# VectorE adds and masks the slot numbers, one operation a pair, and TensorE sums them two units earlier

## The reference

```
off = xn @ W_off + b_off ; w = softmax(xn @ W_attn + b_attn over 4 points)   # 8 heads x 4 points
idx = clip(off as an index into 128 features of the sequence's first token)
attention = broadcast(sum over heads and points of x0[idx] * w) @ W_out + b_out
ffn = sum over 2 shared experts of (silu(x w1) * (x w3)) w2
    + sum over the token's best 2 of 8 routed experts, weighted by a softmax of their two logits
```

## Time and profile before

| | us |
|---|---|
| median of three runs | 412.9 |
| the profiled execution's own time | 413.27 |
| its span | 411.3 |
| TensorE busy in the span | 367.9 |
| VectorE busy | 317.6 |
| ScalarE busy | 189.0 |
| GpSimd busy | 225.8 |

### The profile page before, as it was taken

The page is one execution under the profiler, slowest core; times in us unless marked ns, Lnnn a source line. Parts: engine busy times, 40 slices in busy tenths (PEclk is TensorE's granted clock), DMA queues, the critical chain, the costliest instruction groups (busy, mean ns, idle before and its releaser), DMA issues.

```text
span 411.3 us, 12487 instructions
## 1 busy us (share of the span) xinstructions
PE 367.9 (89%) x4333; PEld 317.0 (77%) x4333; DVE 317.6 (77%) x864; ACT 189.0 (46%) x446; POOL 225.8 (55%) x184
## 2 busy tenths in 40 slices
PE   0067798889999999999999999999999999999992
PEld 0065565467667777777779999999999999999992
DVE  5978989977966799999996778866666666666662
ACT  2778728395432466667666444322222222222220
POOL 0434500403777777343301999448876667766676
PEclk9999999899999999999999999999999999999998
DMA  8944630000117299988885456686854654543233
GB/s 291 297 112 103 119 89 0 2 0 16 49 53 150 73 182 184 171 167 178 141 124 102 121 180 175 164 77 72 76 60 58 60 74 57 61 56 35 27 34 33
DMA packets 98870, 41.35 MB, mean 101 GB/s; under 512 B 73600, under 2 KB 92416, under 8 KB 98816
## 3 DMA queue, kind: packets, MB, share of 16 engines
q1 hardware_dynamic: 87120, 31.82, 38.0%
q0 software_dynamic: 11264, 8.69, 16.5%
q10 hardware_dynamic: 432, 0.11, 0.2%
HBM read 10.93 MB, written 12.88 MB: 58 GB/s over the span
## 4 chain that ended last, share of the span: by engine, by line
PE 75%; DVE 11%; ACT 5%; DMA 3%; issue 2%; SPq 2%; POOL 1%; POOLq 0%; DVEq 0%; ACTq 0%
PE pY L835 18%; PE pY L668 11%; PE pAB L811 8%; PE pAB L810 8%; PE pAB L809 8%; PE pAB L656 5%; PE pAB L658 5%; PE pAB L657 5%; PE pV L680 3%; ACT units L888 2%; PE pV L626 2%; ACT wsp L960 2%; DVE hbuf L1226 1%; DVE hot L1132 1%; DMA xT<-hot 1%
## 5 line engine op out<-in xcount | busy, mean ns | idle before, releaser
L1084 POOL DMA_INDIRECT out_dram<-xT,rows x64 | 99.2, 1551 | 47.8 <-DVE xT L1574 22.9
L1072 POOL DMA_INDIRECT sorted_rows<-rows,slot x64 | 66.8, 1043 | 59.1 <-issue 33.0
L1033 ACT ACTIVATE units<-pAB 128x512 f32<-128x512 f32 x78 | 46.4, 595 | 110.4 <-PE pAB L811 110.4
L810 PE MATMUL pAB<-rows,wsp 128*128 128x128 f16 x512 | 87.6, 219 | 0.0
L811 PE MATMUL pAB<-rows,wsp 128*128 128x128 f16 x512 | 87.6, 219 | 0.0
L809 PE MATMUL pAB<-rows,wsp 128*128 128x128 f16 x512 | 87.6, 219 | 0.0
L1512 DVE SCALAR_TENSOR_TENSOR hbuf<-pAB,units 128x512 f32<-128x512 f32 x78 | 53.5, 686 | 37.9 <-PE pAB L811 37.6
L835 PE MATMUL pY<-wsp,hbuf 128*128 (+1 forms) x620 | 79.1, 279 | 0.4 <-issue 0.4
L835 PEld LDWEIGHTS pY<-wsp,hbuf 128*128 128x128 f32 x620 | 72.9, 192 | 1.0 <-issue 0.9
L668 PE MATMUL pY<-wsp,hbuf 128*128 128x128 f32 x512 | 70.5, 281 | 0.0
L668 PEld LDWEIGHTS pY<-wsp,hbuf 128*128 128x128 f32 x512 | 64.6, 192 | 4.2
(11 more groups left out here) (164 smaller groups left out, 617.2 us busy)
## 6 DMA issues: line engine op xcount, KB each, us to landing
base<-in_x SPq DMA_DIRECT2D x8, 512.0 KB, 7.1
out_dram<-base SPq DMA_DIRECT2D x16, 256.0 KB, 2.5
wraw<-in_wall SPq DMA_DIRECT2D x10, 256.0 KB, 3.0
rows<-hot SPq DMA_DIRECT2D x8, 256.0 KB, 2.8
proj<-sorted_rows SPq DMA_DIRECT2D x27, 68.5 KB, 1.9
wsp<-in_wall SPq DMA_DIRECT2D x10, 128.0 KB
sorted_rows<-rows,slot POOLq DMA_INDIRECT x64, 2.4
out_dram<-xT,rows POOLq DMA_INDIRECT x64, 3.3
```

The lines of the kernel that those rows point to most:

```text
L810: pe.matmul(o, hi, x(1), start=False, stop=False)
L1033: nc.scalar.activation(silu[:, q % 2, 0:job.cols], pAB[:, 2 * (q % 2), 0:job.cols], ACT.Silu, scale=1 / (XS * WS)).then_inc(d_silu, 1)
L1072: pool.indirect_dma_start(sorted_rows, bass.IndirectOffsetOnAxis(ap=slot[:, t:t + 1].bitcast(U32), axis=0), rows[:, t, :], None, bounds_ch ...
L1084: pool.indirect_dma_start(out_rows, bass.IndirectOffsetOnAxis(ap=meta[:, t, DEST - CW:DEST - CW + 1].bitcast(U32), axis=0), yt[:, t], None ...
```

## The change

VectorE does the add and the multiply in one scalar_tensor_tensor a pair: `(scan + seg) * paired`. The 28 operations stand behind hf 12, 14 on each side of hf 13, and the second half signals `place_ready`. ScalarE's 28 adds, VectorE's one large multiply and the semaphore `offset_added` go. TensorE's `PLACE_UNIT` goes from 16 to 14. Because one more `shared_unit()` stands ahead of the rest of VectorE's list, everything from L1325 on comes one unit later there.

```diff
-GAP_UNIT, SEG_UNIT, TAB_UNIT, PLACE_UNIT, TABLE_UNIT = 7, 11, 13, 16, 17
-OFFSET_UNIT, LOGIT_UNIT, ABS_UNIT, WHOLE_UNIT, SIGN_UNIT = 12, 15, 16, 17, 18
+GAP_UNIT, SEG_UNIT, TAB_UNIT, PLACE_UNIT, TABLE_UNIT = 7, 11, 13, 14, 17
+LOGIT_UNIT, ABS_UNIT, WHOLE_UNIT, SIGN_UNIT = 15, 16, 17, 18
...
-        offset_added = sem("offset_added")
...
-                for half in range(2):
-                    if n == OFFSET_UNIT + half:
-                        act.wait_ge(cw_part, 2)
-                        act.wait_ge(offset_ready, 1)
-                        for a in range(NPAIR // 2 * half, NPAIR // 2 * (half + 1)):
-                            ins = nc.scalar.activation(place[:, a, :], scan[:, a, :], ACT.Identity, bias=seg[:, 0, a:a + 1])
-                        ins.then_inc(offset_added, 1)
...
             v.tensor_copy(tab16[:], tab_f[:, 0:2]).then_inc(tab_ready, 1)
 
             shared_unit()
+            dve.wait_ge(offset_ready, 1)
+            dve.wait_ge(cw_part, 2)
+            for half in range(2):
+                for a in range(NPAIR // 2 * half, NPAIR // 2 * (half + 1)):
+                    ins = v.scalar_tensor_tensor(place[:, a, :], scan[:, a, :], seg[:, 0, a:a + 1], paired[:, a, :], ALU.add, ALU.mult)
+                if half:
+                    ins.then_inc(place_ready, 1)
+                else:
+                    shared_unit()
 
             v.tensor_tensor(weight4, weight4, wide4(wmax[:, 0]), ALU.subtract).then_inc(logit_ready, 1)
             shared_unit()
...
             shared_unit()
-            assert unit[0] > OFFSET_UNIT + 1
-            dve.wait_ge(offset_added, 2)
-            v.tensor_tensor(place, place, paired, ALU.mult).then_inc(place_ready, 1)
-
             assert unit[0] >= TAB_UNIT
             dve.wait_ge(tab_done, 1)
```

## The result

The kernel after takes **429.16 us** (428.51 to 430.25, four runs) against 413.03 for the kernel before on the same chip: a ratio of 1.0393, 95% interval 1.0369 to 1.0416. The forecast was slower, 421.7, with a range that ended at 424.0. So the direction held and the size did not.

A forecast was written before the change was run, and what follows sets the result against it. TensorE was taken as the bound, three quarters of the chain that ended last. Slot copy 8.15 later, less 1.03 slack, plus 1.7 for the clock: 8.8 us later, 421.7 us against 412.9; range 416.5 to 424.

The forecast's parts named there:

- The price of one operation: Each new VectorE scalar_tensor_tensor takes 0.20 us (0.10 to 0.246): 14 in 2.8 us, all 28 in 5.6.
- The first wait: TensorE idles 3.9 us ahead of the slot products at unit 14, until VectorE's second group of operations ends.
- the second: TensorE's second new wait: the table products wait 4.4 us for the slots, until about 105.5.
- What is queued behind the sums: Silu 15 and the exponentials come after TensorE's sums; silu 15 to silu 16 takes 5.13 us on ScalarE.
- The clock: TensorE's clock falls behind the first new wait, on the slot products, costing 1.7 us as behind the wait at 71.4.
- 8.15: VectorE's slot copy comes 8.15 us later, at 105.3 instead of 97.15, and the sorted rows' landing moves equally.
- The second fall: A clock fall behind the table products' wait is hidden but for some 0.3 us.
- The sort: The sorted rows' landing moves by 8.15, delaying unit 37 by 7.1 us, more than TensorE's own 5.7.
- the slack of 1.03: Before the change, hf 35 ends at 144.40 and unit 37's first products need it at 145.49: 1.03 us to spare.
- The clock did fall: Rival, clock does not fall behind the first new wait: same waits without the 1.7, +7.1, 420.0 us; chance 0.23.
- the operation was not cheap: Rival, new VectorE operation is cheap: 0.14 us each, first wait 2.2 us, 418.3 us; chance 0.20.
- nothing was faster: Rival, faster: exponentials done before TensorE's sums, no second wait; at 0.10 an operation 411.4 us; chance 0.04.

The follow-up runs named there:

- the first experiment: The changed kernel with 16 unused dense 128x512 half-precision products in TensorE's wait ahead of the slot products: 422.08 us, ratio 1.0214.
- the two kernels above: Kernel before with three unneeded tiles sent ahead of the second sort, 416.76 us; changed kernel reordered, four groups of seven operations, sums and exponentials at 16, 412.16 us.
- the last version: The reordered changed kernel with VectorE's split of the low part moved ahead of the operation waiting for the second sort: 412.64 us, ratio 0.9991.
- the one before it: Changed kernel reordered: operations in four groups of seven, sums and exponentials at unit 16, slot copy ahead of VectorE's weight sums: 412.16 us, ratio 0.9986.

## Why the prediction was right in direction and wrong in size

- **The price of one operation: right.** 0.20 us each, as taken (14 in 2.82). The estimate by the Trainium skill, "VectorE: DVE Perf Modes", in its section on the trn2 errata, 0.13 us, does not agree with this trace; the measured 0.20 decides. That the forecast hit it is in part luck: the row with the scalar operand reads one of its tensors from TensorE's accumulator (xT<-pY), and the new operation does not.
- **The first wait: right**, 3.74 for 3.9; so is the second, 4.29 for 4.4.
- **What is queued behind the sums: right.** Silu 15 to silu 16 is 5.13 us, as before, and silu 15 comes first when the sums are over. Moving the exponentials took 2.9 us off.
- **The clock: this is the step that failed.** "[...] a loss of 4.12 x 0.41 = 1.7 us. My first new wait is longer, so I expect the same behind it, on the slot products, straight on the path." The term measured 6.5: 5.58 on the slot products and 0.92 on the second products of unit 11. The mistake is in the row that it was priced by. Behind the wait at 71.4 stand first products of a unit, and the clock is back within the 4.12 us; I took what the fall cost there as a property of the fall. Behind the new wait stand 56 small products' records instead, and the clock stayed at its lower level to their end. With dense products behind the wait, the sums at 16, the fall did cost 1.6. The first experiment takes 7.1 us away with no order or wait changed, and the products set into the middle of the sums show that it was what TensorE ran, and not the time since the wait, that kept it low. With 6.5 for 1.7 the sum is 8.15 - 1.03 + 6.5 = 13.6, which gives 426.9 from the profiled 413.27; the 2.6 from there to 429.52 are the 1.25 that was there before the change begins and the waits further on.
- **The second fall: right that it is hidden.** It cost TensorE 1.7 us in the kernel after and more in the first experiment: there, from the table products at 105.85 to the second products at 110.94, 5.09 us go by where the same work takes 0.44 + 0.89 + 1.29 = 2.6 at full clock (table products, second products, first products, from start to start), 2.5 lost. In both that only used up what the sort had to spare: unit 37 is set by the landing in both.
- **The sort: right, but with hardly anything to spare.** The landing moved by 15.73 with the slot copy (15.94), and unit 37 behind it by 14.70, which is 15.73 less the slack of 1.03. TensorE had by then lost 14.49 itself, so the sort decided by 0.21 where 1.4 had been forecast. In the first experiment the landing moved by 9.12 and unit 37 by 8.09, with 7.84 lost by TensorE itself. What I did not see is the second way from that wait to TensorE, through the transposes, which cost 1.2 us in the two kernels above and 1.48 in the first experiment.
- **The rivals.** The clock did fall, the operation was not cheap, and nothing was faster. The range ended at 424 because its upper end varied only the operation's price and left the clock at a single row's value.

What stays open: why the same kernel takes one of two times, with the sums at 15, with the small products in the wait and, once in four, with the sums at 16. A clock that falls in some executions only would explain it, and the trace of the second has such a fall, but no kernel was traced in both. Open too is what in the sums' products leaves the clock low: they are narrow, in fp32 and each with a weight load, and no run takes these apart.

## What to carry to other kernels

Read what the engine runs next behind a new wait before you price the wait: here 3.7 us of idling cost 3.7 us and then 6.5 more, because the first thing behind it was a long run of small products during which TensorE's clock stayed at 1.2 GHz. If the order allows it, let dense products stand behind the wait (the fall cost the sums at 16 and the first products ahead of them 1.6 us, where it cost the sums at 14 and the second products behind them 6.5), or fill it. And look at every instruction queued behind a wait for a transfer, not only the one that names it: a delay reached TensorE a second time through transposes that were issued late.

## What the runs showed of the hardware

- The granted clock stayed at 0.50 through 11.85 us of back-to-back 128x64 f32 products, and was back 4.5 us after the first of ten 128x512 f16 products set among them. Products of the first kind ran 6.3 us at 1.00 behind waits of 0.55 us (the kernel before) and 1.36 (the sums at 15).
- A fall shows in the wait or just behind it: with a wait of 3.74 us 0.2 us after its end (the kernel after), with one of 3.86 1.6 us before it (the exponentials at 14).
- It also fell without a long wait: at 88 us in the run with small products in the wait, in the midst of them, with 0.88 us of idling before; in three of five executions of that kernel the time says that it did not.
- Behind the same wait of 2.5 us that the forecast took its price from, the clock fell in twelve of the fourteen traces and stayed at 1.00 in two (the exponentials at 14, and the last version). In these two TensorE came from unit 11 to unit 12 in 2.6 us instead of the 3.6 to 4.2 of the others, but then waited 0.4 and 0.8 for VectorE, and at unit 14 next to nothing of it was left (82.95 us in the last version, 83.03 in the one before it). So that fall, from which the price was taken, cost these kernels hardly any time: VectorE decided there.
- Useless products in an idle stretch made a kernel 7.1 us faster, and ten of them in the middle of the sums, 4.27 us on the path, made it no slower (428.63 and 429.16).
- A product of the sums leaves two records (28 and 56; 16 and 32 in the run with small products). That fp32 alone makes them two, as told above of the kernel before, does not fit its second products, which are in fp32 too and leave eight for eight.
